# Bank 4 shared by two score products, output transposes first in a group, bursts of second scores of 3, 4 and 3

## The chip, the cores and the metric

The kernel runs on 1 core of one Trainium2 chip. The metric is the device time of one execution in microseconds (us). All arithmetic, inputs and outputs are float32 unless said otherwise. PE is TensorE, DVE VectorE, ACT ScalarE, POOL GpSimd and SP SyncE.

## The reference

Two layers over x of 4 batches, 512 tokens and 512 features. The change lies in the attention of the first layer, beside which the experts of the first layer's gate run:

```
x  = L0_attn_x                                   # (4, 512, 512)
xn = layernorm(x)
# attention: 32 heads of 16, 8 groups of keys and values (4 heads share one)
q, k, v = xn @ wq, xn @ wk, xn @ wv ; q, k rotated (rope)
scores = q k^T / sqrt(16) + causal mask
s = softmax(scores) v @ wo
# experts: each token's two best of 8
top_idx = top_k(xn @ W_gate + b_gate, 2)
g = silu(mean over the two of relu(xn @ W_e + b_e))
x = x + s * g
# second layer: an S4 convolution of 512 taps over the feature axis, times silu of a scaled linear layer
xn = layernorm(x)
x = x + s4(xn) * silu(xn @ w_deq^T + bias)
```

## The kernel before

The program has three stages. The first makes the layer norm, the projections and the routing of tokens to 39 expert tiles of 128 rows. The second, in which the change lies, runs attention group by group: a group (b, h) is one of 4 batches and one of 8 key-value heads with its 4 query heads, 32 groups in all. I number them 0 to 31 (8b + h). The third stage is the second layer.

**Scores are made twice.** *First scores* have queries as rows; VectorE adds the mask and takes each row's maximum (`maxima`, line 1400). These maxima are copied (`maxima_columns`, line 1409), turned by TensorE (`turn_maxima`, line 1640, "the turn"), split in two parts on VectorE (`maxima_rows`, lines 1417 and 1419) and stored as two more rows of the query operand. *Second scores* have keys as rows, with the maximum already subtracted in the product; ScalarE takes their exponentials (`exps`, line 1523), GpSimd clears what the causal mask excludes in diagonal blocks (`select`, line 1338), and TensorE multiplies with the values (`values`, line 1657).

A group has ten first scores (n = 0 to 9, line 1601) and ten second scores (n = 0 to 9, lines 1627 and 1630), each of them 512 columns into one PSUM bank. First score n is followed by maximum n, second score n by exponential n. A product uses 48 or 50 rows of the array, in one half of it or the other by n's parity, so that two products can run side by side; they are issued in turns, a first score of the *next* group and a second score of this one.

**Banks.** There are eight of 128 x 512. First scores rotate through three (0, 1, 5), second scores through three (2, 3, 6). Bank 4 takes the value products of a group and, in between, the turned maxima; bank 7 takes the expert and output products. First score n waits for maximum n - 3 and second score n for exponential n - 3, the readers of its bank.

**One group on TensorE**, written out in `pe_b`: burst one of first scores 3 to 6 of the next group with second scores 0 to 3 of this one; the quarters of gap 0; burst two of first scores 7 to 9 with second scores 4 to 6; up to three quarters of gap 1; the turn; the rest of gap 1; burst three of first scores 0 to 2 of the group after next with second scores 7 to 9; gap 2; the value products; gap 3. A *quarter* is one of four products of an expert tile (line 1685) or of an output tile (line 1696), two instructions. The numbers of quarters in the four gaps are (2, 4, 2, 0), (2, 3, 1, 0) or (2, 2, 2, 0) (`SIZES`).

**One group on VectorE**, in `dve_b`: maxima 3 to 6; the output transpose of the group before this one (`rows_of`, line 1430: it reads bank 4, where that group's value products have ended; it signals `b_o`); where h = 0 its division here (`divided`, lines 1435, 1439, 1447); maxima 7 to 9; the copy for the turn; elsewhere the division here; the two instructions behind the turn; then *expert transposes* (`expert_x`, line 1465, slot 0; each turns one tile of gathered token rows for its quarters); maxima 0 to 2 of the group after next; a piece of the S4 preparation (`dve_s4`); expert transposes of slot 1. The tables `TURNS` and `WORK` give the tiles: slot 1 holds one expert transpose in 17 of groups 1 to 29, two in groups 5, 10, 13, 18, 21 and 27, and none in the others.

**One group on ScalarE**, in `act_b`: exponentials 0 to 3, the eviction of a tile that ended in gap 0, exponentials 4 to 6, and so on. Every engine runs its own list in order and waits on semaphores: `b_m` counts maxima, `b_e` exponentials, `b_o` output transposes, `b_pv` the steps of value products.

## Time and profile before

| what | us |
| --- | --- |
| median of 3 runs | 658.91 |
| lowest and highest | 658.34, 660.49 |
| the profiled execution's own time | 656.67 |
| its span in the trace | 654.9 |
| TensorE busy, of the span | 605.2 |
| VectorE busy | 549.0 |
| ScalarE busy | 285.9 |

The profiled execution is one by itself, a little under the fastest of the timed runs; what is read from its trace is to be set against its own 656.67. The views of the trace used below give, for one stretch of time, each instruction or a few of a kind merged (with start and length), who waited for whom, and the busy time of each engine. An instruction whose idle time is shown in brackets was waited for by its engine, and the name behind the arrow is what released it.

### The profile page before, as it was taken

How to read it: one execution, taken by the hardware profiler on the slowest of the kernel's cores; microseconds unless marked ns; L12 is line 12 of the kernel's file. 1: busy time of each engine (PE TensorE's matmuls, PEld its weight loads, DVE VectorE, ACT ScalarE, POOL GpSimd, SP SyncE). 2: the span in 40 equal slices, each digit the busy share in tenths (PEclk: the TensorE clock that was granted, in tenths of full speed). 3: DMA queues.
4: the chain of work that ended last, by engine and by line, in shares of the span. 5: the costliest groups of instructions: out<-in, count | busy, mean ns of one | idle time of the engine just before them, and what ended most of it. 6: DMA issues, size and time to landing. Idle time of an engine off the chain costs nothing.

```text
span 654.9 us, 12411 instructions
## 1 busy us (share of the span) xinstructions
PE 605.2 (92%) x3541; PEld 348.9 (53%) x3565; DVE 549.0 (84%) x1789; ACT 285.9 (44%) x535; POOL 238.3 (36%) x364
## 2 busy tenths in 40 slices
PE   8899998968889999999999999998999999699997
PEld 5788784424444434444444444444444443388886
DVE  6698999867989979978988888997899957589994
ACT  4344324333345444534444534544454443445441
POOL 2767641332223133323221332212232116576620
PEclk9999999959999999999999999999999999889999
DMA  7599987665868643656742465644266328668841
GB/s 265 139 333 272 338 247 175 151 192 163 258 190 253 166 133 87 163 152 174 199 140 78 120 168 167 172 130 130 81 161 185 130 67 243 139 160 221 193 112 65
DMA packets 82880, 113.13 MB, mean 173 GB/s; under 512 B 12680, under 2 KB 45640, under 8 KB 82816
## 3 DMA queue, kind: packets, MB, share of 16 engines
q1 hardware_dynamic: 71074, 86.91, 44.8%
q0 software_dynamic: 6704, 18.62, 12.3%
q10 hardware_dynamic: 5038, 6.84, 4.2%
q8 instruction: 29, 0.48, 0.3%
q14 instruction: 35, 0.29, 0.2%
HBM read 72.15 MB, written 39.65 MB: 171 GB/s over the span
## 4 chain that ended last, share of the span: by engine, by line
PE 64%; DVE 20%; DMA 4%; issue 4%; POOL 2%; SPq 2%; ACT 2%; ACTq 1%; DVEq 0%; POOLq 0%
PE bank L1685 17%; DVE bank L1400 10%; PE bank L1027 8%; PE bank L1657 8%; PE bank L1601 7%; PE bank L2174 7%; PE bank L1696 5%; PE bank L2179 4%; DMA w_e<-expert_rows,slots 3%; PE bank L1627 2%; PE bank L1004 1%; DVE arena L1400 1%; ACTq L1321 1%; DVE arena L1465 1%; PE bank L2163 1%
## 5 line engine op out<-in xcount | busy, mean ns | idle before, releaser
L1400 DVE CUSTOM_DVE_ANT_0 bank<-bank,cst 128x384 f32<-128x384 f32 (+3 forms) x512 | 233.9, 522 | 37.5 <-PE bank L1601 35.1
L1523 ACT ACTIVATE arena<-bank 128x512 f32<-128x512 f32 x320 | 169.6, 602 | 147.8 <-PE bank L1627 113.9
L1338 POOL TENSOR_SCALAR_AFFINE_SELECT arena<-arena 128x512 f32<-128x512 f32 x128 | 80.5, 641 | 301.0 <-ACT arena L1523 301.0
L1685 PE MATMUL bank<-w_e,arena 128*128 x312 | 151.1, 609 | 7.5 <-DVE arena L1465 3.8
L1601 PE MATMUL bank<-kt,qt 48*128 48x512 f32 (+1 forms) x496 | 108.3, 336 | 13.1 <-DVE arena L1400 13.0
L1601 PEld LDWEIGHTS bank<-kt,qt 48*128 48x128 f32 x496 | 67.7, 187 | 80.2 <-DVE arena L1400 44.3
L1627 PE MATMUL bank<-qt,kt 50*128 50x512 f32 x256 | 93.7, 449 | 0.8 <-ACT arena L1523 0.4
L1685 PEld LDWEIGHTS bank<-w_e,arena 128*128 128x128 f32 x312 | 55.9, 192 | 52.0 <-issue 48.2
L1657 PE MATMUL bank<-arena 128*32 128x512 f32 (+3 forms) x1024 | 77.7, 441 | 0.0
L1400 DVE DVE_READ_ACCUMULATOR2_ANT arena<- 128x1 f32 x512 | 71.9, 140 | 0.0
L1696 PE MATMUL bank<-w_proj,arena 128*128 128x512 f32 x128 | 64.6, 629 | 0.8 <-ACT s_tok L1514 0.8
L1657 PEld LDWEIGHTS bank<-arena 128*32 128x32 f32 x1024 | 28.5, 110 | 50.5 <-issue 42.3
L1533 ACT ACTIVATE arena<-bank 128x512 f32<-128x512 f32 x39 | 23.4, 599 | 66.5 <-PE bank L1685 66.4
L1627 PEld LDWEIGHTS bank<-qt,kt 50*128 50x128 f32 x256 | 44.4, 186 | 4.7 <-ACT arena L1523 3.3
L1027 PE MATMUL bank<-proj_high,xh 128*128 128x264 f32 (+1 forms) x128 | 46.2, 361 | 0.4 <-DVE xl L527 0.4
L1027 PE MATMUL bank<-proj_low,xh 128*128 128x264 f32 (+1 forms) x128 | 43.5, 339 | 0.0
L1027 PE MATMUL bank<-proj_high,xl 128*128 128x264 f32 (+1 forms) x128 | 43.5, 339 | 0.0
L859 POOL TENSOR_TENSOR s_tok<-arena 128x256 f32<-128x256 f32 (+1 forms) x64 | 33.6, 555 | 25.8 <-DVE arena L546 20.2
L1350 POOL DMA_INDIRECT s_tok<-xn_rows,slots_i x39 | 38.1, 978 | 10.2 <-issue 5.2
L1696 PEld LDWEIGHTS bank<-w_proj,arena 128*128 128x128 f32 x128 | 22.5, 195 | 24.7 <-issue 20.5
L1924 POOL DMA_INDIRECT w_e<-expert_rows,slots x16 | 27.4, 1710 | 13.7 <-DMA w_e<-expert_rows,slots 10.5
L542 DVE TENSOR_TENSOR arena<-bank,cst 128x128 f32<-128x128 f32 (+1 forms) x63 | 27.1, 475 | 5.0 <-PE bank L1027 4.7
(168 smaller groups left out, 942.0 us busy)
## 6 DMA issues: line engine op xcount, KB each, us to landing
qt<-turned_parts SPq DMA_DIRECT2D x192, 64.0 KB, 2.7
turned_parts<-qk_parts SPq DMA_DIRECT2D x8, 1280.0 KB, 6.6
gathered_rows<-s_tok SPq DMA_DIRECT2D x39, 256.0 KB, 3.6
arena<-gathered_rows SPq DMA_DIRECT2D x39, 256.0 KB, 4.0
expert_rows<-arena SPq DMA_DIRECT2D x39, 256.0 KB, 2.3
w_e<-in_L_ffn_W_e ACTq DMA_DIRECT2D x24, 256.0 KB, 6.0
kt<-turned_parts SPq DMA_DIRECT2D x180, 32.0 KB, 2.7
arena<-in_L_attn_x SPq DMA_DIRECT2D x16, 256.0 KB, 6.0
```

Source lines behind the costliest of these rows:

```text
L859: i = g.tensor_tensor(o[:, :, :, c, :], xc[:, :, :, c, :], xs[:, :, :, 1 - c, :], op)
L1027: i = t.matmul(out[u % 2][:, 0:n], x[:, u % 2, k, :], w[part][:, k, :], start=(k == 0 and x is xh and part == 0), stop=(k == KB - 1 and pa ...
L1338: g.affine_select(out=diag, in_=diag, compare_op=ALU.is_ge, fill=0.0, base=0, pattern=[[0, 2], [0, HALF], [1, P]], channel_multiplier=-1). ...
L1350: e.indirect_dma_start(xr[m % 3], None, xn_d, bass.IndirectOffsetOnAxis(ap=slots_i[:, m:m + 1], axis=0)).then_inc(m_x[m % 3], 16)
L1400: i = v.tensor_tensor_reduce(out=part, in0=part, in1=const("mask")[:, S - w:], scale=1.0, scalar=LOWEST, op0=ALU.add, op1=ALU.max, accum_o ...
L1523: nc.scalar.activation(pt[:, s, first:second + 1:second - first].rearrange("p c r q -> p c (r q)"), s2_bank(b, h, n).rearrange("p (c x) -> ...
L1601: i = t.matmul(s1_bank(b, h, n)[:, at:at + w], stack[rows, x if r is None else r, q * P:w], kt[rows, h // 2 % 2, h % 2, 0:w], start=(x == ...
L1627: i = t.matmul(to, keys(j), queries[:, q:q + 2], start=True, stop=True)
L1657: i = nc.tensor.matmul(bank[4][VW * r:VW * (r + 1), j * P:], vb[:, j, h, :], pt[:, r // HALF, at:at + TPB - j, r % HALF, :], start=(j == O ...
L1685: i = t.matmul(bank[7], xgt[:, m % 2, k * P:(k + 1) * P], w_e[:, ex[m], k, :], start=False, stop=(k == KB - 1))
L1696: i = t.matmul(bank[to], ot[:, (b * PAIRS + k) % (PAIRS + 1), u, :], wo[:, k, :], start=(k == 0), stop=(k == KB - 1))
L2174: i = t.matmul(bank[2 + u % 2][:, :], x[:, u % 2, k, :], (w_high, w_low)[part][:, k, :], start=(k + n == 0), stop=(k + n == KB + 1))
```

## The change

Five edits, all in the second stage.

- First score 6 of a group (from the third group on) is written to bank 4 and no longer to its rotating bank. It waits for `b_o`, the output transpose of two groups back, in place of a maximum. The other first scores rotate over three banks without it, so those after it wait for maximum n - 4 in place of n - 3 (first scores 7 to 9), which in the rotation is again the reader of their bank.
- Second score 6 (in all groups but the first and the last) is written to bank 4 as well. It waits for maximum 6 of the next group. The second scores after it wait for exponential n - 4.
- The turn, which is written to bank 4 too, waits for exponential 6 besides.
- On VectorE the output transpose and behind it the expert transposes of the last group's slot 1 stand ahead of maxima 3 to 6. They stood behind maximum 6, and at the end of the last group.
- Second score 3 moves from burst one to burst two. ScalarE's eviction of the first gap's tile moves ahead of exponential 3.

```diff
         def s1_bank(b, h, n):
 
-            return S1_BANK[1 if (b, h) == (0, 0) else nth_of(NJ, b, h, n) % 3]
+            if (b, h) == (0, 0):
+                return S1_BANK[1]
+            if (b, h) == (0, 1):
+                return S1_BANK[(n + 1) % 3]
+            return bank[4] if n == 6 else S1_BANK[(n + 2 - (n > 6)) % 3]
 
         def s2_bank(b, h, n):
 
-            return S2_BANK[n % 2 if (b, h) == (0, 0) else nth_of(NJ, b, h, n) % 3]
+            if (b, h) == (0, 0):
+                return S2_BANK[n % 2]
+            if (b, h) == LAST_GROUP:
+                return S2_BANK[n % 3]
+            return bank[4] if n == 6 else S2_BANK[(n - (n > 6)) % 3]
...
+                    done, later = next_group(b, h, -1), h > 0 and following
+                    rows_of(*done)
+                    for m in TURNS.get((*done, 1), ()):
+                        expert_x(m)
                     if following:
                         for n in (3, 4, 5, 6):
                             maxima(e, *following, n)
-                    done, later = next_group(b, h, -1), h > 0 and following
-                    rows_of(*done)
                     if not later:
                         divided(*done)
...
-                    for m in TURNS.get((b, h, 1), ()):
-                        expert_x(m)
...
-                    for n in (0, 1, 2, 3):
+                    for n in (0, 1, 2):
                         exps(e, b, h, n)
                     results(b, h, 0)
-                    for n in (4, 5, 6):
+                    for n in (3, 4, 5, 6):
                         exps(e, b, h, n)
...
+        def second_burst(e, g1, g2):
+
+            scores_2(e, *g2, 3)
+            scores_2(e, *g2, 4)
+            scores_1(e, *g1, 7)
+            scores_1(e, *g1, 8)
+            scores_2(e, *g2, 5)
+            scores_2(e, *g2, 6)
+            scores_1(e, *g1, 9)
...
-            elif due(at := nth_of(NJ, b, h, n if alone_in_bank else n - 2)):
+            elif n == 6 and b * NG + h > 1:
+                e.wait_ge(b_o, nth_of(1, b, h, -1))
+            elif due(at := nth_of(NJ, b, h, n if alone_in_bank else n - 2 - (n > 6 and b * NG + h > 1))):
                 e.wait_ge(b_m, at)
...
-            elif due(at := nth_of(NJ, b, h, n - (1 if (b, h) == (0, 0) else 2))):
+            elif n == 6 and (b, h) not in ((0, 0), LAST_GROUP):
+                e.wait_ge(b_m, nth_of(NJ, b, h, NJ + 7))
+            elif due(at := nth_of(NJ, b, h, n - (1 if (b, h) == (0, 0) else 2) - (n > 6 and (b, h) not in ((0, 0), LAST_GROUP)))):
                 e.wait_ge(b_e, at)
...
             if due(at := nth_of(1, b, h, -1)):
                 e.wait_ge(b_o, at)
+            if b * NG + h > 1:
+                e.wait_ge(b_e, nth_of(NJ, b, h, 7 - NJ))
             t.transpose(turned_at(b, h), m_cols.rearrange("p s c x -> p (s c x)"), ident).then_inc(b_tm, 1)
...
-                    scores(e, (3, 4, 5, 6), following, (0, 1, 2, 3), (b, h))
+                    scores(e, (3, 4, 5, 6), following, (0, 1, 2), (b, h))
                     quarters(b, h, 0)
-                    scores(e, (7, 8, 9), following, (4, 5, 6), (b, h))
+                    second_burst(e, following, (b, h))
```

VectorE's order at the start of group 11, before. Line 671 is the end of group 10's S4 piece, line 1465 the expert transposes, the rows of line 1400 the maxima 3 (512 wide), 6 (384 and 128) and 7, line 1430 the output transpose; the rows left out are the readings and maxima 4 and 5:

```order
L671 TENSOR_TENSOR w_proj<-toep,arena 128x256 x2
L1465 STREAM_TRANSPOSE arena<-arena 128x4x4x32 x2
L1400 ISA bank0,arena<-bank0,cst 128x512
...
L1400 ISA bank0,arena<-bank0,cst 128x384
L1400 ISA arena 128x1
L1400 ISA bank0,arena<-bank0,cst 128x128
...
L1430 STREAM_TRANSPOSE arena<-bank4 128x512
L1400 ISA bank1,arena<-bank1,cst 128x384
```

The same place after the change, where line 1409 is what line 1400 was, 1439 the output transpose and 1474 the expert transposes:

```order
L671 TENSOR_TENSOR w_proj<-toep,arena 128x256 x2
L1439 STREAM_TRANSPOSE arena<-bank4 128x512
L1474 STREAM_TRANSPOSE arena<-arena 128x4x4x32 x2
L1409 ISA bank5,arena<-bank5,cst 128x512
...
L1409 ISA bank4,arena<-bank4,cst 128x384
L1409 ISA arena 128x1
L1409 ISA bank4,arena<-bank4,cst 128x128
...
L1409 ISA bank5,arena<-bank5,cst 128x384
```

The output transpose moved from behind maximum 6 to the front, and the two expert transposes now stand behind it; maximum 6 reads bank 4.

TensorE's order in group 11 before, from first score 6 on (line 1601; names ending in 67 are bank 6 or 7). Lines 1627 and 1630 are second scores, 1696 the two quarters of gap 0:

```order
L1601 MATMUL bank0<-kt,qt_56 128x384
L1601 MATMUL bank0<-kt,qt_56 128x128
L1627 MATMUL bank67<-qt_56,kt 128x512
L1696 MATMUL bank67<-w_proj,arena 128x512 x2
L1601 MATMUL bank1<-kt,qt_56 128x384
L1601 MATMUL bank1<-kt,qt_56 128x128
L1627 MATMUL bank2<-qt_56,kt 128x512
L1601 MATMUL bank5<-kt,qt_56 128x256 x2
L1627 MATMUL bank3<-qt_56,kt 128x512
L1601 MATMUL bank0<-kt,qt_56 128x256 x2
L1630 MATMUL bank67<-qt_56,kt 128x256 x2
```

The same place after, where 1601 is 1622, 1627 is 1650, 1630 is 1653 and 1696 is 1721:

```order
L1622 MATMUL bank4<-kt,qt_56 128x384
L1622 MATMUL bank4<-kt,qt_56 128x128
L1721 MATMUL bank67<-w_proj,arena 128x512 x2
L1650 MATMUL bank2<-qt_56,kt 128x512
L1650 MATMUL bank3<-qt_56,kt 128x512
L1622 MATMUL bank5<-kt,qt_56 128x384
L1622 MATMUL bank5<-kt,qt_56 128x128
L1622 MATMUL bank0<-kt,qt_56 128x256 x2
L1650 MATMUL bank67<-qt_56,kt 128x512
L1653 MATMUL bank4<-qt_56,kt 128x256 x2
L1622 MATMUL bank1<-kt,qt_56 128x256 x2
```

First score 6 and second score 6 now write bank 4, second score 3 stands in burst two, and second score 6 stands ahead of first score 9.

## Rows read from the trace of the kernel before

**Rows 1.** Stretches: length; busy PE, PEld, DVE, ACT, POOL; granted clock; DMA.

```profile
129.60:134.10 4.50, 3.63 (x22) 2.22 (x21) 4.50 (x19) 3.10 (x6) 1.58 (x2) 1.00 0.66 176
134.10:147.70 13.60, 8.14 (x30) 3.14 (x33) 6.94 (x26) 2.28 (x4) 3.77 (x5) 0.50 0.74 209
150.70:539.30 388.60, 361.76 (x2190) 171.09 (x2212) 340.91 (x1280) 179.50 (x342) 106.55 (x152) 1.00 0.53 153
```

**Rows 2.** Waits of 150.7 to 539.3: us in total, times, longest.

```profile
PE bank L1601 <- DVE arena L1400: 12.5, 29, 1.2
...
PE bank L1640 <- DVE arena L1409: 4.5, 12, 0.7
```

**Rows 3.** Timeline of TensorE, group 17: start, length, what, [idle before <- releaser].

```profile
354.07 0.51 PE L1657 MATMUL bank<-arena 128*32 128x384 f32 x4
354.51 0.49 PE L1601 MATMUL bank<-kt,qt 48*128 48x512 f32 x1
...
355.85 0.45 PE L1601 MATMUL bank<-kt,qt 48*128 48x384 f32 x1 [0.32 <-DVE arena L1400]
...
356.14 0.22 PE L1601 MATMUL bank<-kt,qt 48*128 48x128 f32 x1
356.28 1.98 PE L1696 MATMUL bank<-w_proj,arena 128*128 128x512 f32 x4
358.20 0.44 PE L1601 MATMUL bank<-kt,qt 48*128 48x384 f32 x1
...
358.54 0.44 PE L1627 MATMUL bank<-qt,kt 50*128 50x512 f32 x1
...
358.79 0.28 PE L1630 MATMUL bank<-qt,kt 50*128 50x256 f32 x1
...
358.94 0.27 PE L1601 MATMUL bank<-kt,qt 48*128 48x256 f32 x1
359.36 2.74 PE L1685 MATMUL bank<-w_e,arena 128*128 x6 [0.16 <-issue]
361.94 0.27 PE L1640 MATMUL bank<-cst,arena 128*128 128x128 f32 x1
```

**Rows 4.** Timeline of VectorE, the same group.

```profile
355.04 0.70 DVE L1400 CUSTOM_DVE_ANT_0 bank<-bank,cst 128x512 f32<-128x512 f32 x1 [1.46 <-PE bank L1601]
355.65 0.14 DVE L1400 DVE_READ_ACCUMULATOR2_ANT arena<- 128x1 f32 x1
...
357.95 0.14 DVE L1400 DVE_READ_ACCUMULATOR2_ANT arena<- 128x1 f32 x1
357.95 0.71 DVE L1430 STREAM_TRANSPOSE arena<-bank 128x512 f32<-128x512 f32 x1
358.73 0.57 DVE L1400 CUSTOM_DVE_ANT_0 bank<-bank,cst 128x384 f32<-128x384 f32 x1
...
361.17 0.18 DVE L1409 COPY arena<-arena 128x32 f32<-128x32 f32 x1
```

**Rows 5.** Timeline of TensorE in group 8: the start of burst one, and the turn.

```profile
232.85 0.50 PE L1601 MATMUL bank<-kt,qt 48*128 48x512 f32 x1
...
241.16 0.33 PE L1640 MATMUL bank<-cst,arena 128*128 128x128 f32 x1 [0.71 <-DVE arena L1409]
```

**Rows 6.** Timeline of VectorE at the start of group 11 (burst one at 272.01).

```profile
271.13 1.30 DVE L1465 STREAM_TRANSPOSE arena<-arena 128x512 f32<-128x512 f32 x2
```

**Rows 7.** Timeline of VectorE: maximum 7 in groups 6 (start 206.09) and 18 (366.39).

```profile
210.45 0.57 DVE L1400 CUSTOM_DVE_ANT_0 bank<-bank,cst 128x384 f32<-128x384 f32 x1 [0.21 <-PE bank L1601]
...
370.73 0.57 DVE L1400 CUSTOM_DVE_ANT_0 bank<-bank,cst 128x384 f32<-128x384 f32 x1
```

**Rows 8.** Timeline of VectorE in group 8: the division, and maximum 7.

```profile
237.15 0.26 DVE L1435 RECIPROCAL arena<-arena 128x16 f32<-128x16 f32 x1
...
238.53 0.53 DVE L1400 CUSTOM_DVE_ANT_0 bank<-bank,cst 128x384 f32<-128x384 f32 x1
```

**Rows 9.** The page: ScalarE's exponentials, busy us and mean ns of one.

```profile
L1523 ACT ACTIVATE arena<-bank 128x512 f32<-128x512 f32 x320 | 169.6, 602 | 147.8 <-PE bank L1627 113.9
```

1 line of the change is left out of this document (added).

## The prediction

> **What bounds the kernel now.** The page's busy shares say that TensorE and VectorE are the two full engines, and little more, so I read the stretches first: of the 388.6 us in which groups 2 to 30 run, TensorE is busy 361.8 and VectorE 340.9 [rows 1]. So both are nearly full there, and what counts is who waits for whom. The waits of that stretch name two places [rows 2]: a first score waits for VectorE's maxima in each of the 29 groups (12.5 us in all, at most 1.2), and the turn of the maxima waits 12 times (4.5 us). Then I laid one group out on both engines. I count time in a group from the start of its burst one; for group 17 that is 354.51 [rows 3], and "at 1.34" is meant so. It stands for the groups whose pace TensorE sets.
>
> Group 17 on TensorE [rows 3]: the value products of the group ahead end at 0.07, first score 6 starts at 1.34 after 0.32 idle, two quarters at 1.77, burst two at 3.69, its last product starts at 4.43, the next quarter at 4.85, the turn at 7.43. On VectorE [rows 4]: maximum 3 starts at 0.53, the last reading of maximum 6 ends at 3.58, the output transpose runs 3.44 to 4.15, maximum 7 starts at 4.22, the copy that the turn needs ends at 6.84. The turn comes 0.59 after it: here TensorE sets the pace. In group 8 (h = 0) the turn waits 0.71 for the copy [rows 5], and in groups with two quarters in gap 1 (6, 14, 18 and others) it waits less: there VectorE sets it.
>
> **What the change removes.** First score 6 waits for the output transpose in place of maximum 3. That transpose can start when the value products are done. VectorE started 0.04 after the TensorE result it needed (355.00 to 355.04), so at 0.11; it takes 0.71, end 0.82 [rows 3, 4]. TensorE answered VectorE's maximum 3 (355.79) after 0.06, so first score 6 starts at about 0.87 instead of 1.34. From there it is 0.43 to the quarters and 1.92 to burst two [rows 3], which so starts at 3.22 instead of 3.69. It has seven products now, not six; six took 0.74 from first start to last, half a pair more costs some 0.21, and the last would start at 4.17 instead of 4.43. **If nothing else waited, 0.26 us a group would be gained.** That second score 3 leaves burst one saves nothing, since it ran beside first score 6 and the quarters followed the latter.
>
> **What it adds.** Second score 6, in burst two, goes to bank 4 as well, and so must wait until VectorE has read first score 6 out of it. Ahead of that maximum VectorE now has the output transpose, and also the expert transposes that stood at the end of the group ahead. These were hidden: in group 11 two of them run 271.13 to 272.43, ahead of the maxima [rows 6]. Now they can't start before the value products end. One transpose lets the next instruction start after about 0.63 (two took 1.30, of which the last one's own 0.67) [rows 6]; from the start of maximum 3 to the last reading of maximum 6 are 3.05 [rows 4]. With x moved transposes, maximum 6 is read at 0.11 + 0.63 + 0.63x + 3.05 = **3.79 + 0.63x**. The product itself would be ready at 3.22 + 0.60 = 3.82. Queued behind it are the last first score, the quarters, the turn and the rest of the group, and VectorE itself waits for that turn; nothing gives the wait back. After a wait the second instruction of a product started 0.29 after the first (355.85, 356.14) [rows 3]. So the last product of burst two starts at 3.79 + 0.63x + 0.05 + 0.29:
> - x = 1: 4.76 against 4.43, a loss of 0.33.
> - x = 2: 5.39, a loss of 0.96.
> - x = 0: the wait is just over; 4.17.
>
> Bounds: with 0.12 in place of the restart of 0.29 (the nearest rows of products that didn't wait lie that close), each TensorE-set group loses 0.17 less; if the moved transpose pays a start of its own after its wait for a load, 0.1 more. I take the 0.29, as the row is of this very case, a product behind a VectorE wait.
>
> Where VectorE sets the turn, maximum 7 counts. It follows the last instruction of maximum 6, 0.08 ahead of the end of its reading, or comes at about 4.0, when its product is there.
>
> **The sum**, with x the number of expert transposes that the plan in the code puts at the end of the group ahead:
> - x = 1 and TensorE sets the turn: groups 5, 7, 9, 12, 13, 17, 20, 21, 23, 25, 29, 30. 12 by 0.33 = +4.0.
> - x = 1, but VectorE late already or setting the turn: 3, 4, 15, 27. In the first two maximum 3 started at 1.29 and 1.08 since the expert transpose was on the path before: 0.13 + 0.11 + 0.23 + 0.12 = +0.6.
> - x = 2 and TensorE sets the turn: 11, 19. 2 by 0.96 = +1.9.
> - x = 2 and VectorE sets it: 6 and 28, where maximum 7 moves from 4.36 [rows 7] to 4.97, +0.61 each; by the same reckoning 14 (from 4.63) +0.34, and 22 (from 5.24, VectorE late already) -0.18. +1.4.
> - x = 0, h = 0: 8, 16, 24. Between the maxima stands the division, 1.42 from one start to the next. Maximum 7 starts at 0.11 + 0.63 + 2.97 + 1.42 = 5.13 instead of 5.68 [rows 5, 8], and the turn had waited for it: 3 by -0.55 = -1.65.
> - x = 0 otherwise: 10, 18, 26. Maximum 7 from 4.34 [rows 7] to about 4.02, when its product is there; in 10 VectorE is free only at 0.24: -0.18 - 0.31 - 0.31 = -0.8.
> - Group 2: its value products end 1.8 ahead of the burst, so all transposes lie in idle time: -0.36. Group 1: the turn is set by VectorE's work, the same in either order: 0. Group 31 has no first scores to wait: 0.
>
> Together 4.0 + 0.6 + 1.9 + 1.4 - 1.65 - 0.8 - 0.36 = **+5.1 us**.
>
> Costed at nothing: the turn now also waits for exponential 6. At x = 2 second score 6 ends at about 5.7 and an exponential takes 0.60 [rows 9], so 6.3, and the turn is at 7.6; with x = 0 all is 1.3 earlier. Each us past the turn would be a us. The eviction of the first gap's tile stands one exponential earlier on ScalarE, and burst two covers it. SyncE's load of the next expert tile waits for the moved transpose, up to 2 us later in the group, and its tile is used a group later. One more wait stands ahead of the turn; it costs between nothing and about 0.1 in the 12 groups where the turn waits for VectorE, and is in the range only.
>
> The profiled execution took 656.67, its span 654.9; with the change that is 661.8. It was 2.2 below the median of the runs shown, so the forecast for a median is 658.91 + 5.1 = **664.0 us**.
>
> On the pairs: pair starts in a burst lie some 0.24 to 0.35 apart [rows 3], and before the change two products in a row often used the same half of the rows; now the halves alternate all through burst two. The Trainium skill ("TensorE: Matmul & The Clock Gate", Part 3, The mechanism) says that weight loads overlap running matmuls only where the row group differs. By that rule the new burst two would close up, by 0.1 a group as my estimate from the 0.34 between its first two pair starts and the 0.24 of the next. In groups with x of 1 or 2 the wait swallows it, so by the rule the sum is 0.6 lower, and by the rows as above.
>
> **Rivals.**
> 1. *The wait for maximum 6 is hidden* (faster). It decides where maximum 6 is read by 3.82 even with x = 1, that is if VectorE is 0.6 quicker than its rows. Then the 12 groups gain 0.26 each (-3.1), 3, 4 and 15 some 0.4 each (-1.2), 11 and 19 lose only 0.2 each at the turn, and the rest stays as above (27 +0.1, x = 2 +1.4, the others -2.8): about -5.2, 653.7 us. For it: the 12.5 us of waiting do go, and VectorE has idle time. Against it: that idle time lies ahead of the value products' end, where the moved transposes can't be any more. 0.10.
> 2. *The same mechanism, smaller.* With 0.12 for the restart in 14 groups (-2.4) and the closer pairs (-0.6), +2: about 661 or less, which is within 0.3%, the least that a measurement of this kernel can tell. 0.16.
> 3. *The clock, or a second wait.* TensorE's granted clock stood at 0.50, its 1.2 GHz level, in 134.1 to 147.7, and TensorE was busy for 8.1 of those 13.6 us, after 3.6 of the 4.5 ahead of them; in groups 2 to 30 it was 1.00 [rows 1]. A second such stretch would cost 4 us (its busy work at full speed took half) to 7 us (half the stretch): 668 to 671. The new wait is a piece of idle of up to 1.3 us. Against it: a wait of 1.2 stood in a group before [rows 2] and the clock held. The Trainium skill ("TensorE: Matmul & The Clock Gate", HAM oscillation) has TensorE's idle between pieces of work bring the clock down; by that rule groups 6, 11, 19 and 28 are where it would show. With other losses as large, such as a GpSimd gather behind a delayed store: 0.14.
>
> **Numbers.** Forecast 0.60, rivals 0.10, 0.16, 0.14. The low end takes in rival 2 and runs as low as the lowest before, 659.5. The high end adds to the forecast 1.2 for the waits, 1.6 by which the highest run of before lies over the median, and 0.8 for the moved transposes' own start: 667.5. Faster 0.10, same 0.16, slower 0.74.
>
> **What would show it.** First scores wait for VectorE's maxima for under 2 us, not 12.5. A new wait stands at second score 6 (line 1653 after) for VectorE: about 0.6 with x = 1, 1.3 with x = 2, some 14 us in all. The turn is at 7.8 in group 17, 8.4 in group 11, 7.8 in group 8. It would be wrong if maximum 6 is read before burst two gets there, if the turn doesn't follow burst two by the same distance, or if something behind the turn waits anew.

## The result, and the profile after

The changed kernel took 666.88 us (median of 4 runs, 666.05 to 668.55) beside 659.20 for the kernel before on the same chip: a ratio of 1.0111, 95% interval 1.0079 to 1.0143. It is slower, as forecast, and 2.9 us above the forecast median of 664.0, inside the range. The profiled execution took 666.05 with a span of 664.3 (656.67 and 654.9 before). Measured twice more, on two chips, the same kernel gave 1.0062 (1.0043 to 1.0080) and 1.0075 (1.0047 to 1.0103); the forecast was 664.0 / 658.91 = 1.0077. So the change itself costs about what was forecast, and the first measurement holds more: some 3 us by the ratio, 3.8 us in its trace, which the sections below place but don't explain.

Lines of the code after stand 9 to 25 further down than before: the maxima are L1409, the output transpose L1439, the expert transpose L1474, the exponentials L1532, a first score L1622, a second score L1650 (512 columns) and L1653 (256 or 128, second score 6 among them), the turn L1665, the value products L1682, the quarters L1710 and L1721.

Stretches of the changed kernel, with the columns of [rows 1]: group 1, and groups 2 to 30.

```profile
131.70:151.70 20.00, 13.22 (x70) 6.20 (x70) 12.15 (x45) 5.33 (x10) 5.34 (x7) 0.74 0.70 192
151.70:547.70 396.00, 373.00 (x2189) 175.20 (x2211) 335.89 (x1279) 179.34 (x341) 106.56 (x152) 1.00 0.52 150
```

The loss is in the second line: 396.00 us where [rows 1] had 388.60, +7.4, at the same granted clock of 1.00. Ahead of it, stage 1 came out 2.1 us longer (untouched work) and group 1 1.1 us shorter; behind it the tail is 1.0 longer. VectorE is busy for 5 us less in a stretch that is 7.4 longer, so it waits more. TensorE is busy for 11.2 us more with the same work. The end of a product is modelled and can cover a part of a wait: second score 6, which starts at 3.90 in groups 8, 16 and 24, which have no moved transposes, starts at 4.49 in group 17, and only 0.15 of that shows as idle (the lines below). So what a wait costs is read here from the starts of instructions, not from busy or idle time.

Waits of 150 to 545 in the changed kernel: us in total, times, longest.

```profile
DVE arena L1439 <- PE bank L1682: 38.7, 26, 4.0
...
PEld bank L1653 <- DVE arena L1409: 13.1, 22, 1.1
...
PE bank L1653 <- DVE arena L1409: 6.2, 22, 0.8
...
PE bank L1622 <- DVE arena L1439: 4.3, 8, 1.2
...
PE bank L1665 <- DVE arena L1418: 2.2, 7, 0.4
```

The 12.5 us in which first scores waited for maxima [rows 2] are gone. Second score 6 (L1653) now waits for maxima in 22 groups: 6.2 us in which TensorE computes nothing, 13.1 us on its weight loads. The prediction's "some 14 us in all" is the row of the weight loads. VectorE waits 38.7 us for value products ahead of the output transpose. And first scores wait 4.3 us for that transpose. By these rows alone TensorE waits less than before (6.2, 4.3 and 2.2 against 12.5 and 4.5), though the stretch is 7.4 longer; that is why the positions within a group follow.

Timelines of group 17, TensorE and then VectorE, to be laid beside [rows 3, 4]; its burst one starts at 359.00.

```profile
359.00 0.50 PE L1622 MATMUL bank<-kt,qt 48*128 48x512 f32 x1
...
360.40 1.99 PE L1721 MATMUL bank<-w_proj,arena 128*128 128x512 f32 x4
362.31 0.50 PE L1650 MATMUL bank<-qt,kt 50*128 50x512 f32 x2
...
363.49 0.38 PE L1653 MATMUL bank<-qt,kt 50*128 50x256 f32 x1 [0.15 <-DVE arena L1409]
...
363.71 0.27 PE L1653 MATMUL bank<-qt,kt 50*128 50x256 f32 x1
...
366.74 0.27 PE L1665 MATMUL bank<-cst,arena 128*128 128x128 f32 x1
```

```profile
359.20 0.72 DVE L1439 STREAM_TRANSPOSE arena<-bank 128x512 f32<-128x512 f32 x1 [1.86 <-PE bank L1682]
359.84 0.67 DVE L1474 STREAM_TRANSPOSE arena<-arena 128x512 f32<-128x512 f32 x1
360.43 0.67 DVE L1409 CUSTOM_DVE_ANT_0 bank<-bank,cst 128x512 f32<-128x512 f32 x1
...
363.30 0.14 DVE L1409 DVE_READ_ACCUMULATOR2_ANT arena<- 128x1 f32 x1
```

Burst two starts at 3.31 (3.69 before), so the old wait is gone. But the transposes push maximum 3 from 0.53 to 1.43, maximum 6 is read at 4.44, and second score 6 starts 0.05 later, at 4.49. The last product starts at 4.71 to 4.73 and the turn at 7.74, against 4.43 and 7.43.

Groups 11 (two moved transposes, burst one at 274.90) and 8 (none, at 235.01) on TensorE: second score 6 and the turn, and the turn alone.

```profile
279.98 0.38 PE L1653 MATMUL bank<-qt,kt 50*128 50x256 f32 x1 [0.76 <-DVE arena L1409]
...
283.22 0.27 PE L1665 MATMUL bank<-cst,arena 128*128 128x128 f32 x1
```

```profile
242.72 0.33 PE L1665 MATMUL bank<-cst,arena 128*128 128x128 f32 x1 [0.38 <-DVE arena L1418]
```

In group 11 the wait is 0.76 and the turn comes at 8.32; in group 8, at 7.71 where [rows 5] had 8.31.

**Six late groups.** Group by group all this agrees with the forecast, except in 5, 10, 13, 18, 21 and 27. There the output transpose starts at 0.55, 1.48, 0.55, 1.43, 0.56 and 0.66 instead of 0.19. Group 10 (burst one at 261.49): VectorE, ScalarE and GpSimd.

```profile
262.96 0.72 DVE L1439 STREAM_TRANSPOSE arena<-bank 128x512 f32<-128x512 f32 x1 [1.24 <-PE bank L1682]
```

```profile
262.98 1.08 ACT L1532 ACTIVATE arena<-bank 128x512 f32<-128x512 f32 x2 [2.63 <-PE bank L1650]
```

```profile
259.91 0.99 POOL L1359 DMA_INDIRECT s_tok<-xn_rows,slots_i  x1 [0.15 <-issue]
261.21 0.95 POOL L1359 DMA_INDIRECT s_tok<-xn_rows,slots_i  x1 [0.30 <-issue]
```

The last value product ended at 261.56, yet VectorE and ScalarE, each released by a different product of TensorE, both started at 262.96 to 262.98. These six are the groups ahead of which GpSimd issues two gathers back to back. "Two in a row" is not the only thing that sets them apart: in the other groups with a gather the last one starts 1.57 us or more ahead of burst one, in these six 0.07 to 1.24, and in all six the output transpose starts 1.5 to 1.8 us after the second gather does (261.21 to 262.96 here). A delay that long behind a gather would be over in the other groups. In the profile of the kernel before there is no such delay in group 10 (burst one at 259.64), where ScalarE and VectorE wait for TensorE too:

```profile
260.21 1.57 ACT L1523 ACTIVATE arena<-bank 128x512 f32<-128x512 f32 x3 [1.71 <-PE bank L1627]
```

ScalarE starts at 0.57 there (1.49 in the changed kernel), and at 0.57 in group 18 (1.44). In the other groups a delay to 0.66 could hardly be seen, and that execution, 656.67 us long, was faster than every timed run of its set (658.34 to 660.49); so it doesn't tell whether the kernel before is free of it.

To compare kernels I use a sum that leaves out groups 2 and 22, the two that change most between executions of one kernel: the lengths of **the 26 groups** 3 to 21 and 23 to 29 (from one burst one to the next). Each sum is from one profiled execution. Groups 3 and 7 still change by up to 0.8 and 0.5 us between executions of one kernel. The 26 groups take 347.15 us in the kernel before and 355.23 in this profile of the changed one.

### The profile page after: what moved, and what is told of

The parts are those of the page before. It is cut to its first block, busy times and chain, and to the rows that moved or that the text cites. A ratio compares the mean times of both kernels' runs of the same rounds, so it can differ in the third digit from the quotient of the medians.

```text
span 664.3 us, 12405 instructions
## 1 busy us (share of the span) xinstructions
PE 617.6 (93%) x3541; PEld 354.5 (53%) x3565; DVE 545.4 (82%) x1789; ACT 286.7 (43%) x535; POOL 239.3 (36%) x364
## 4 chain that ended last, share of the span: by engine, by line
PE 52%; DVE 27%; DMA 7%; issue 6%; POOL 2%; ACT 2%; SPq 2%; ACTq 1%; DVEq 0%; POOLq 0%
DVE bank L1409 14%; PE bank L1710 13%; PE bank L1682 10%; PE bank L2199 7%; PE bank L1027 4%; PE bank L2204 4%; DMA turned_parts<-qk_parts 3%; DVE arena L1474 3%; PE bank L1721 3%; DMA w_e<-expert_rows,slots 3%; PE bank L1622 2%; DVE arena L1409 2%; PE bank L1653 2%; PE bank L983 1%; ACTq L1330 1%
## 5 line engine op out<-in xcount | busy, mean ns | idle before, releaser
L1409 DVE CUSTOM_DVE_ANT_0 bank<-bank,cst 128x384 f32<-128x384 f32 (+3 forms) x512 | 231.7, 520 | 7.1 <-PE bank L1622 6.6
L1532 ACT ACTIVATE arena<-bank 128x512 f32<-128x512 f32 x320 | 169.5, 603 | 150.2 <-PE bank L1650 114.6
L1710 PE MATMUL bank<-w_e,arena 128*128 x312 | 151.2, 609 | 8.0 <-DVE arena L1474 5.0
L1622 PE MATMUL bank<-kt,qt 48*128 48x512 f32 (+1 forms) x496 | 103.3, 333 | 4.3 <-DVE arena L1439 4.3
L1622 PEld LDWEIGHTS bank<-kt,qt 48*128 48x128 f32 x496 | 66.9, 187 | 48.6 <-issue 33.7
L1650 PE MATMUL bank<-qt,kt 50*128 50x512 f32 x256 | 84.1, 449 | 1.0 <-DMA qt<-m_rows 0.5
L1710 PEld LDWEIGHTS bank<-w_e,arena 128*128 128x128 f32 x312 | 55.5, 192 | 53.0 <-issue 49.0
L1682 PE MATMUL bank<-arena 128*32 128x512 f32 (+3 forms) x1024 | 76.6, 436 | 0.0
L1409 DVE DVE_READ_ACCUMULATOR2_ANT arena<- 128x1 f32 x512 | 70.8, 138 | 0.0
L1721 PE MATMUL bank<-w_proj,arena 128*128 128x512 f32 x128 | 64.0, 623 | 0.8 <-ACT s_tok L1523 0.8
L1439 DVE STREAM_TRANSPOSE arena<-bank 128x512 f32<-128x512 f32 x32 | 22.9, 716 | 41.5 <-PE bank L1682 41.4
L1682 PEld LDWEIGHTS bank<-arena 128*32 128x32 f32 x1024 | 28.2, 109 | 49.3 <-issue 41.0
L1650 PEld LDWEIGHTS bank<-qt,kt 50*128 50x128 f32 x256 | 39.2, 186 | 27.4 <-issue 22.7
L1653 PE MATMUL bank<-qt,kt 50*128 50x256 f32 x128 | 31.6, 330 | 7.1 <-DVE arena L1409 6.2
L1721 PEld LDWEIGHTS bank<-w_proj,arena 128*128 128x128 f32 x128 | 22.1, 192 | 24.2 <-issue 20.1
```

The source lines that it names most:

```text
L1409: i = v.tensor_tensor_reduce(out=part, in0=part, in1=const("mask")[:, S - w:], scale=1.0, scalar=LOWEST, op0=ALU.add, op1=ALU.max, accum_o ...
L1532: nc.scalar.activation(pt[:, s, first:second + 1:second - first].rearrange("p c r q -> p c (r q)"), s2_bank(b, h, n).rearrange("p (c x) -> ...
L1622: i = t.matmul(s1_bank(b, h, n)[:, at:at + w], stack[rows, x if r is None else r, q * P:w], kt[rows, h // 2 % 2, h % 2, 0:w], start=(x == ...
L1650: i = t.matmul(to, keys(j), queries[:, q:q + 2], start=True, stop=True)
L1653: i = t.matmul(to[:, x * HALF * P:(x + 1) * HALF * P], keys(j), queries[:, q], start=(x == 0), stop=True, skip_group_check=True)
L1682: i = nc.tensor.matmul(bank[4][VW * r:VW * (r + 1), j * P:], vb[:, j, h, :], pt[:, r // HALF, at:at + TPB - j, r % HALF, :], start=(j == O ...
```

## The experiments

All ratios are to the kernel before on the same chip, which took 656.12 us in the first set, 655.30 in the second, 656.63 in the third and 659.06 in the last.

### The changed kernel again, twice

> The changed kernel itself once more, to see whether what its first trace showed comes again. In that trace groups 2 to 29 took 7.4 us more than before, and 4 of them stood in six groups (5, 10, 13, 18, 21, 27) in which the signal of the last value product reached VectorE 0.3 to 1.3 us late, so that the output transpose started at 0.55, 1.48, 0.55, 1.43, 0.56 and 0.66 of the group and not at 0.20. Theory A (the delay belongs to the program: GpSimd issues two gathers back to back at the end of exactly the groups ahead of these six): the same six groups show the same starts to within 0.1 us, and the time is 666 to 668 us. Theory B (a chance of that execution): other groups or none, and groups 2 to 29 then take 3.5 us more than before and not 7.4.

Measured: 660.90 us, ratio 1.0062 (1.0043 to 1.0080). The output transposes of the six groups start at 0.19 to 0.27; the 26 groups take 351.36 us. Groups 2 to 29 took 5.3 us more than before, where theory B had 3.5. The difference is group 2, 15.05 us long at a lower clock (see the last section) where the later profile has 13.37.

> The changed kernel unchanged, once more. Its first measurement gave a ratio of 1.0111 [1.0079, 1.0143] and a profile with six groups in which the output transpose began 0.3 to 1.3 us late; its second 1.0062 [1.0043, 1.008] and a profile with none of the six. Reading one (chance of an execution or a day's chip): ratio 1.005 to 1.008, groups 2 to 29 at 378 to 380 us, no late start in the six, perhaps one elsewhere. Reading two (belongs to the change, met in some executions): ratio 1.009 to 1.012 and late starts again in those same groups, groups 2 to 29 at 381 us or more.

Measured: 660.68 us, ratio 1.0075 (1.0047 to 1.0103), the six at 0.19 to 0.28, the 26 groups 351.48. Here is group 10 of the later profile (burst one at 260.42), VectorE, ScalarE, GpSimd:

```profile
260.70 0.72 DVE L1439 STREAM_TRANSPOSE arena<-bank 128x512 f32<-128x512 f32 x1
```

```profile
260.99 1.57 ACT L1532 ACTIVATE arena<-bank 128x512 f32<-128x512 f32 x3 [1.71 <-PE bank L1650]
```

```profile
258.85 0.99 POOL L1359 DMA_INDIRECT s_tok<-xn_rows,slots_i  x1 [0.15 <-issue]
260.15 0.95 POOL L1359 DMA_INDIRECT s_tok<-xn_rows,slots_i  x1 [0.30 <-issue]
```

The two gathers lie where they did, within 0.01 us of burst one, and nobody is late. So the gathers alone don't make it (something else must differ between the measurements), and the late starts were 3.8 us of the first profile's 26 groups (355.23 against 351.4). The change's own cost there is 351.4 - 347.15 = +4.3.

### The expert transposes back at the group's end

```diff
                     rows_of(*done)
-                    for m in TURNS.get((*done, 1), ()):
-                        expert_x(m)
...
                         numerators(e, st, h - 2)
+                    for m in TURNS.get((b, h, 1), ()):
+                        expert_x(m)
```

> The change with one part undone: the expert transposes of slot 1 stand again at the end of their group; the output transposes stay ahead of the maxima. Theory 1 (the prediction: they hold back maximum 6 and with it second score 6, on which the rest of the group waits): where x was 1 or 2 maximum 6 is read at about 3.85 and not at 4.43 and 5.02, second score 6 starts at 3.9, and by the same reckoning groups 2 to 30 take 7 us less than the changed kernel: 660 us, as before the change or 0.6 over it, if the value products' signals stay late in six groups, and 656 if they don't. Rival (what costs is bank 4 and its waits, whoever stands ahead on VectorE): at most 2 us less than the changed kernel, 665 to 667 us.

Measured: 654.45 us, ratio 0.9963 (0.9936 to 0.9990); the 26 groups 342.21 us, 9.2 less than the changed kernel and 4.9 less than before. Group 17 (burst one at 353.31), TensorE:

```profile
357.14 0.50 PE L1653 MATMUL bank<-qt,kt 50*128 50x256 f32 x2
...
360.55 0.27 PE L1665 MATMUL bank<-cst,arena 128*128 128x128 f32 x1
```

The whole time is 6.5 us less than the changed kernel's and 1.7 less than before (medians of the same set). The ten runs of this kernel had a mean granted clock of 0.981 and the 19 of the kernel before 0.986, so part of what the groups gain seems to be lost again to more time at the lower clock; why there is more of it is open.

No idle time of TensorE is left ahead of second score 6, which starts at 3.84 right behind the reading of maximum 6 (3.79). The turn comes at 7.25. The steps of the forecast for x = 0 (3.79, turn some 0.26 earlier than 7.43) hold for the groups that TensorE sets and that had one moved transpose (turn at 7.23 to 7.27, in 29 at 7.34). In 11 and 19, which had two, these now end only after burst one has begun, the output transpose starts at 0.34 and the turn comes at 7.39. The place of the expert transposes is necessary for the loss as the change stands.

### The gather later in GpSimd's queue

```diff
+                    if b * NG + h > 0:
+                        next_gather(*next_group(b, h, -1), 2)
                     next_gather(b, h, 0)
...
-                    next_gather(b, h, 2)
```

> The changed kernel with GpSimd's gathers that stood behind the last select of a group now behind the first select of the next one, at 1.8 to 4 of a group, far from the value products. Theory A (two gathers in a row while VectorE stands waiting for the value products' signal hold TensorE's signals back): no output transpose starts later than 0.25 except where VectorE is late by itself (groups 3 and 4), groups 10 and 18 are 1.2 us shorter each, 5, 13, 21 by 0.35 and 27 by 0.45, together 4 us: 662.5 to 663.5 us. Theory B (the lateness has another cause): the six late starts stay, 666 to 668 us. If the later gathers hold up GpSimd's selects or a load of an expert tile, another group gets longer.

Measured: 669.85 us, ratio 1.0189 (1.0162 to 1.0215), but for a reason of its own: the first gathers are late, and group 1 waits for its expert tile (27.14 us long instead of 19.90). The stretch 130.00 to 151.20 in this kernel, then in the changed kernel's second profile, columns as in [rows 1]:

```profile
130.00:151.20 21.20, 7.68 (x39) 4.20 (x39) 10.70 (x43) 5.55 (x10) 7.44 (x9) 0.68 0.56 152
```

```profile
130.00:151.20 21.20, 14.89 (x80) 6.94 (x80) 12.93 (x48) 5.83 (x12) 5.35 (x7) 0.76 0.72 190
```

As no late start was met on that chip in any kernel, it says nothing of the late starts. A wasted run: the control should have been seen to be late first.

### The wait of the output transpose in two instructions

```diff
-                e.wait_ge(b_pv, nth_of(4, b, h, 4))
                 if due(at := nth_of(1, b, h, 0)):
                     e.wait_ge(b_on, at)
+                alone(e)
+                e.wait_ge(b_pv, nth_of(4, b, h, 4))
```

`alone` is a nop that keeps the wait ahead of it out of the next instruction.

> The changed kernel with one edit on VectorE: the wait ahead of the output transpose, which in the trace is one instruction that stands waiting for two semaphores (the value products' and VectorE's own), is split, so that the transpose carries the wait for the value products alone. Theory A1 (it is this standing double wait, together with the gathers, that holds TensorE's signals back): the starts of the output transposes in groups 5, 10, 13, 18, 21 and 27 go to 0.2, 662.5 to 663.5 us; all others start 0.05 to 0.1 earlier too. Theory A2 (the gathers do it with any kind of wait): the six stay late, 666 to 668 us.

Measured: 662.44 us, ratio 1.0077 (1.0050 to 1.0103), the same as the changed kernel in the whole time. In the trace the transposes start at 0.14 instead of 0.19, the turn of group 17 at 7.67 instead of 7.73, and the 26 groups take 350.45 instead of 351.4. So the split is worth 0.05 us in those groups. It isn't a price that every wait for two semaphores pays: with the wait unsplit the transpose starts at 0.14 too in group 30 of the changed kernel, and in x_back's groups that have one expert transpose just ahead of it (17, for one). In groups 3, 4, 10 and 22 the split made it 0.10 later.

### The second scores' old banks, with the rest of the change

```diff
         def s2_bank(b, h, n):
-            if (b, h) == (0, 0):
-                return S2_BANK[n % 2]
-            if (b, h) == LAST_GROUP:
-                return S2_BANK[n % 3]
-            return bank[4] if n == 6 else S2_BANK[(n - (n > 6)) % 3]
+            return S2_BANK[n % 2 if (b, h) == (0, 0) else nth_of(NJ, b, h, n) % 3]
...
-            elif n == 6 and (b, h) not in ((0, 0), LAST_GROUP):
-                e.wait_ge(b_m, nth_of(NJ, b, h, NJ + 7))
```

> The changed kernel, but the second scores keep the three banks in turn that they had before the change, so second score 6 waits for an exponential and not for maximum 6. All else of the change stays: first score 6 in the value products' bank, output and expert transposes ahead of the maxima, bursts of 3, 4 and 3. Theory (the loss is the wait of second score 6 for maximum 6): with that wait gone the twelve groups with one expert transpose have their last product of burst two at 4.2 to 4.3 us and the turn of the maxima at 7.25 to 7.3 instead of 7.73, groups 11 and 19 the turn at 7.3 to 7.5 instead of 8.33; groups 2 to 29 take about 370 us instead of 379.5 (374.3 in the kernel before), and the time is 8 us or more under the changed kernel's 660.9, some 652 to 654 us. Rival A (VectorE's longer work before maximum 3 is itself the cost, since later maxima run late): the turn stays at 7.6 or later and the time within 2 us of 660.9. Rival B (the exponential becomes the new wait of second score 6): a wait of the second scores for ScalarE of more than 5 us over groups 2 to 29, and groups 2 to 29 at 374 to 377 us.

Measured: 660.39 us, ratio 1.0070 (1.0042 to 1.0099); the 26 groups 351.20. My theory, as I put it there, fell, and rival B's wait is in the trace: 6.1 us, groups 2 to 29 in 377.70 (B had up to 377). Rival A's two numbers came out as well (turn at 7.79, time within 2 us); against it speaks that the turn still comes 3.01 after the last product of burst two, so that VectorE's later maxima don't set it. The waits of 150 to 545, group 17 on TensorE (burst one at 358.88), and ScalarE there:

```profile
PEld bank L1647 <- ACT arena L1528: 15.2, 29, 0.5
...
PE bank L1647 <- ACT arena L1528: 6.1, 29, 0.2
```

```profile
363.43 0.39 PE L1647 MATMUL bank<-qt,kt 50*128 50x256 f32 x1 [0.23 <-ACT arena L1528]
...
366.67 0.27 PE L1657 MATMUL bank<-cst,arena 128*128 128x128 f32 x1
```

```profile
362.29 0.59 ACT L1519 COPY s_tok<-bank 128x512 f32<-128x512 f32 x1 [1.27 <-PE bank L1713]
362.78 2.07 ACT L1528 ACTIVATE arena<-bank 128x512 f32<-128x512 f32 x4
```

With three banks in turn, second score 6 takes the bank of second score 3. Before the change these two were in different bursts; now they are in the same one, so TensorE has to wait until exponential 3 has read the bank, and that exponential can only follow its own product in the same burst: it starts at 3.90, 0.59 after second score 3 (3.30), where exponential 0 starts 0.57 after second score 0. The eviction ahead of it (362.29) therefore costs 0.03 at most. Second score 6 starts at 4.55, no earlier than with its wait for maximum 6 (4.49).

### The new bursts alone

The kernel before, with bursts of 3, 4 and 3 second scores and the eviction ahead of exponential 3; on TensorE:

```diff
-                    scores(e, (3, 4, 5, 6), following, (0, 1, 2, 3), (b, h))
+                    scores(e, (3, 4, 5, 6), following, (0, 1, 2), (b, h))
                     quarters(b, h, 0)
-                    scores(e, (7, 8, 9), following, (4, 5, 6), (b, h))
+                    second_burst(e, following, (b, h))
```

> The kernel before with one part of the change alone: bursts of 3, 4 and 3 second scores instead of 4, 3 and 3, so second score 3 moves from burst one to burst two, and on ScalarE the evacuation of results goes ahead of exponential 3. Banks and VectorE's order are those of before. It tells what the seventh product of burst two costs by itself, which my sum had at 0.21 us. Theory (burst one is filled by its wait for the output transpose, so a product taken out of it gives nothing back, and the seventh in burst two costs 0.21 in each group that TensorE sets, 12 to 17 of them): +2.5 to +3.5 us. Rival (first score 6 starts by as much earlier as burst one is shorter, the two cancel): 0 within 1 us.

Measured: 673.17 us, ratio 1.0271 (1.0223 to 1.0319); the 26 groups 360.54, +13.4, where both theories had 3.5 or less. Group 17 on TensorE (burst one at 361.31):

```profile
366.25 0.38 PE L1640 MATMUL bank<-qt,kt 50*128 50x256 f32 x1 [0.23 <-ACT arena L1523]
...
369.50 0.27 PE L1650 MATMUL bank<-cst,arena 128*128 128x128 f32 x1
```

The same wait for exponential 3: second score 6 at 4.94 instead of 4.28, the turn at 8.18 instead of 7.43. So moving second score 3 with the other edits left out costs 0.75 a group, not 0.21, and the bank that the change gives second score 6 is what pays for it. The exponential again starts 0.59 after its product (4.28 and 3.69), so the moved eviction isn't the reason.

### Both put back: the fourth corner

The two diffs above together: expert transposes at the group's end, second scores in their old banks.

> The changed kernel with the expert transposes back at the end of the group and, with that, the second scores in the three banks in turn of before. With the kernel after, the expert transposes alone put back (groups 2 to 29 in 370.9 us) and the banks alone put back (377.7) it makes a square of four. New theory (two waits stand side by side at second score 6: maximum 6 if it goes to the value products' bank, exponential 3 if it shares a bank with second score 3, which now is in the same burst; the later one decides): second score 6 at 4.5 to 4.55 us in the groups that TensorE sets although maximum 6 is read at 3.79, last product at 4.75, turn of the maxima at 7.75 to 7.8, and groups 2 to 29 at 376 to 378 us, time 659 to 661; nothing of the 8.6 us that the expert transposes gave back alone. Rival (the exponential was late only because maximum 3 and what follows were late): second score 6 at 3.9 to 4.1, groups 2 to 29 at 370 to 372 us, time 653 to 655.

Measured: 662.74 us, ratio 1.0085 (1.0052 to 1.0119); the 26 groups 351.59. Group 17 (burst one at 358.13), TensorE:

```profile
362.63 0.38 PE L1647 MATMUL bank<-qt,kt 50*128 50x256 f32 x1 [0.22 <-ACT arena L1528]
...
365.87 0.27 PE L1657 MATMUL bank<-cst,arena 128*128 128x128 f32 x1
```

Second score 6 at 4.50 and the turn at 7.73, although the transposes are out of the way. The whole time and groups 2 to 29 (380.23) lie 2 us over the forecast; group 22, which the sum leaves out, took 15.23 at a lower clock. The square, in us for the 26 groups:

| | second score 6 in the value products' bank | old banks in turn |
|---|---|---|
| expert transposes ahead of the maxima | 351.4 (the change) | 351.2 |
| at the group's end | **342.2** | 351.6 |

Of two waits at one instruction the later decides. They happen to end within 0.06 us of each other (4.49 and 4.55), so taking away either alone gives nothing, and the 9 us of these groups (6.5 in the whole time) come only where both are short. The ratios of the four say the same: 1.0062 and 1.0075, 1.0070, 0.9963, 1.0085.

### x_back with the split wait

> The changed kernel with the expert transposes back at the end of the group, and with the wait for the value products in an instruction of its own, so that the output transpose has one semaphore to wait for and not two. The expert transposes at the group's end alone gave 654.45 us, a ratio of 0.9963 to the kernel before, and groups 2 to 29 at 370.9 us. Theory: the split starts the output transpose 0.05 us earlier in each group (0.14 to 0.09, or 0.14 still if that is already when the signal comes), which moves maximum 6, second score 6 and the turn by as much in the twelve groups that TensorE sets: 0 to -0.6 us, a ratio of 0.995 to 0.9965. Rival (the added instruction delays VectorE elsewhere): +1 us or more.

Measured: 653.43 us, ratio 0.9963 (0.9939 to 0.9987); the 26 groups 342.07 against 342.21. The groups that TensorE sets had their output transpose at 0.14 already; only groups without moved transposes (8, 16, 18, 24, 26) gain their 0.05.

### VectorE's wait for the value products in the kernel before

```diff
+                    prior = next_group(b, h, -1)
+                    e.wait_ge(b_pv, nth_of(4, *prior, 4))
+                    if due(at := nth_of(1, *prior, 0)):
+                        e.wait_ge(b_on, at)
+                    alone(e)
                     if following:
                         for n in (3, 4, 5, 6):
                             maxima(e, *following, n)
```

> The kernel before, with VectorE waiting ahead of maximum 3 of each group for the value products' signal and for the evacuation of results, although maximum 3 needs neither. It tells apart two readings of the late starts that one profiled execution of the changed kernel had in groups 5, 10, 13, 18, 21 and 27 and a later execution had not. Reading one (TensorE's signals of the value products come late by chance, and in the kernel before nothing stood behind them at that place): single groups begin maximum 3 0.3 to 1.3 us later than 0.53, in some executions. Reading two (late signals belong to the change's own order): no group is late. The price of the wait with every signal on time is 0 to 0.05 us a group, under 1.5 us in all, because maximum 3 waits for its scores until 0.53 anyway.

Measured: 654.93 us, ratio 0.9990 (0.9962 to 1.0018), the 26 groups 346.54 against 347.15: such a wait costs nothing when the signals are on time. No group was late, but that chip had no late starts in any kernel, so this leaves the question open.

### The best version: two parts of the change alone

The kernel before, with the output transpose first (its wait split as above) and first score 6 in the value products' bank. Bursts, second scores' banks, ScalarE's order and the expert transposes as before:

```diff
+            return bank[4] if n == 6 else S1_BANK[(n + 2 - (n > 6)) % 3]
...
+                    done, later = next_group(b, h, -1), h > 0 and following
+                    rows_of(*done)
                     if following:
                         for n in (3, 4, 5, 6):
                             maxima(e, *following, n)
-                    done, later = next_group(b, h, -1), h > 0 and following
-                    rows_of(*done)
...
+            elif n == 6 and b * NG + h > 1:
+                e.wait_ge(b_o, nth_of(1, b, h, -1))
...
```

> The kernel before with two parts of the change alone: the output transpose first in the group (with the wait for the value products in an instruction of its own), and first score 6 in the value products' bank. Bursts of 4, 3 and 3, the banks of the second scores, the order on ScalarE and the place of the expert transposes are those of before. Theory: first score 6 starts at 0.91 instead of 1.34, all of burst two comes 0.43 earlier (start 3.26, last product 4.00), no second score waits for a maximum or for an exponential of its own burst, and the turn comes at 7.02 instead of 7.43 in the groups that TensorE sets, 0.21 earlier than with x_back (7.23); VectorE could be ready at 4.02 + 2.67 = 6.69. Groups 2 to 29: 370.9 less 12 to 14 times 0.21, so 368 us, time 650 to 652, a ratio of 0.990 to 0.993, the fastest so far. Rival (VectorE or the exponentials become the bound before the turn, the seventh product of burst two was hidden): turn at 7.2 or later, groups 2 to 29 at 370.5 to 372, a ratio of 0.996.

Measured: 650.89 us, ratio 0.9909 (0.9874 to 0.9943): the time that the theory named, with a mechanism that was wrong in one step. The turn of group 17 comes at 7.32, not 7.02, and the 26 groups take 342.61. TensorE there (burst one at 354.65):

```profile
355.87 0.50 PE L1635 MATMUL bank<-qt,kt 50*128 50x512 f32 x1
356.30 1.98 PE L1704 MATMUL bank<-w_proj,arena 128*128 128x512 f32 x4
358.21 0.44 PE L1609 MATMUL bank<-kt,qt 48*128 48x384 f32 x1
...
361.97 0.27 PE L1648 MATMUL bank<-cst,arena 128*128 128x128 f32 x1
```

The quarters start at 1.65. In the kernel before it took 0.43 from first score 6 to them, here 0.74: second score 3 (355.87) used to fill the 0.29 between the two pieces of first score 6 after its wait [rows 3], and without the wait there is no such gap. So second score 3 costs 0.31 in burst one here, and the new bursts with bank 4 are worth only 0.07 to 0.09 a group (turn at 7.23 to 7.25 against 7.32). By the 26 groups this version and x_back are equal within 0.5 us; by their intervals (0.9874 to 0.9943, and 0.9936 to 0.9990) I can't call it faster.

> The same kernel as in the run named old_bursts (output transpose first, first score 6 in the value products' bank, all else as before), once more with five rounds. It measured 0.9909 [0.9874, 0.9943] there, and the two with the expert transposes put back 0.9963 with intervals that end at 0.9936 and 0.9939. By groups 2 to 29, and leaving out the groups 2 and 22, the three take as long as each other within 1 us, so the theory is that the true ratio lies between: 0.990 to 0.995, groups 2 to 29 at 369 to 370 us, the turn of the maxima at 7.31 again. Rival (the first measurement had luck): 0.995 to 0.998.

Measured on a fourth chip: 655.26 us, ratio 0.9916 (0.9889 to 0.9944), against 659.06 for before; groups 2 to 29 in 373.58, where 369 to 370 was expected. Both measurements lie below 1 with all of their intervals: output transpose first and one bank changed are worth 0.6 to 1.3%. And on this chip the late starts are back, in the same six groups: 0.50, 1.39, 0.46, 1.39, 0.55 and 0.63 in groups 5, 10, 13, 18, 21 and 27. Group 10 (burst one at 261.13), VectorE, ScalarE and GpSimd:

```profile
262.52 0.72 DVE L1436 STREAM_TRANSPOSE arena<-bank 128x512 f32<-128x512 f32 x1 [1.15 <-PE bank L1665]
```

```profile
262.58 0.60 ACT L1529 ACTIVATE arena<-bank 128x512 f32<-128x512 f32 x1 [2.59 <-PE bank L1635]
```

```profile
259.56 0.99 POOL L1355 DMA_INDIRECT s_tok<-xn_rows,slots_i  x1 [0.15 <-issue]
260.86 0.95 POOL L1355 DMA_INDIRECT s_tok<-xn_rows,slots_i  x1 [0.30 <-issue]
```

This kernel has neither the moved expert transposes, nor the new bursts, nor the second scores' new bank. So the late starts don't need those, and a chance of single executions is unlikely: the same six groups, in two kernels, in the first measurement and on this chip, and in none of the ten profiles on the three chips between that could have shown them. Here too the output transpose starts 1.5 to 1.8 us after the second gather does. In the two sets that show them the kernel before took 659.2 and 659.1 us, in the others 655.3 to 656.6, so it is some 3 us slower there as well. What delays these starts on such a chip is open; so is whether the kernel before loses its 3 us by the same, since its waiting variant wasn't run on such a chip.

## Why the prediction was right, point by point

**The bound, and the wait that goes.** Right: first scores no longer wait for maxima, burst two starts at 3.31 (I had 3.22). The term was 0.09 off, since the output transpose starts at 0.19 and not at 0.11. I had taken the 0.04 with which VectorE answered one product of TensorE; here it answered after 0.12, of which splitting the wait in two instructions took away 0.05.

**The wait that comes.** Right in place and mechanism: second score 6 for maximum 6, in 22 groups. 3.79 + 0.63x gave 4.42 for x = 1, read 4.44; for x = 2, 5.05, read 5.03. Two errors cancel: the start was 0.08 later, the transposes 0.64 and 0.59 apart and the maxima 0.04 shorter. The restart was 0.23 and not 0.29, so the last product starts at 4.72 (4.76 forecast) and 5.31 (5.39). Without the wait (x = 0) maximum 6 was read at 3.84 and the last product started at 4.28, where I had 4.17.

**The sum**, from the changed kernel's third profile, which has no late starts, as the change of the turn against the kernel before (groups 2 and 4: of the length):

| groups | forecast each | measured each |
|---|---|---|
| x = 1, TensorE sets the turn (12) | +0.33 | +0.28 to +0.30, in 30 +0.21 |
| 11, 19 (x = 2) | +0.96 | +0.85, +0.88 |
| 6, 28 | +0.61 | +0.56, +0.57 |
| 14; 22 | +0.34; -0.18 | +0.29; -0.29 |
| 8, 16, 24 | -0.55 | -0.60 |
| 10; 18 and 26; 2 | -0.18; -0.31; -0.36 | -0.18; -0.25; -0.35 |
| 15; 3; 4; 27 | +0.23; +0.13; +0.11; +0.12 | +0.17; +0.04; +0.02; +0.10 |

That adds up to +3.7 us where the forecast had +5.1; the whole lengths of groups 2 to 29 differ by +3.7 (377.96 against 374.28). That the turn follows burst two at a fixed distance was right: 3.00 before, 3.01 after. In 8, 16 and 24 the forecast used 1.42 from one start to the next over the division; [rows 8] give 238.53 - 237.15 = 1.38, and with that the term is -0.59, as measured.

**What the sum missed.** The first measurement's +7.4 in groups 2 to 30 is this +3.7 and the 3.8 of the late starts. I had costed the output transpose's new wait at the plain latency of a signal, because no row of the kernel before had VectorE waiting for TensorE between the gathers and burst one. That the first result lay in the range is luck in this part: the range went up for other reasons (1.2 for waits, 0.8 for the transposes' own start). Its low end of 659.5 is called the lowest before; that was 658.34.

**A step that was right only in company.** The prediction had 0.21 for the seventh product, and nothing saved by second score 3 leaving burst one. The runs show that the move costs 0.75 without the other edits (a wait for exponential 3), that the new bank of second score 6 removes that wait, and that leaving burst one saves 0.31 as soon as first score 6 doesn't wait. None of it changes the sum, as all parts of the change are there at once; but a reader who took the parts for independent would have dropped the bank, and lost 9 us (x_back against the fourth corner, 342.2 and 351.6).

**The rivals.** Rival 1 (the wait hidden) needed x = 0 ahead of the maxima: with the expert transposes back it is what happens, at 654.45. Rival 2 (smaller) is what the two later measurements look like, ratios of 1.0062 and 1.0075, though by other terms than its 0.12 restart. Rival 3 (the clock) didn't decide the first result: the granted clock over groups 2 to 30 was 1.00 after as before. In the second profile a small piece of it is there (group 2).

**On the pairs of scores.** The Trainium skill ("TensorE: Matmul & The Clock Gate", Part 3, The mechanism) led me to expect burst two to close up by 0.1 us a group. Group 2 is where its seven products run without a wait in between (maximum 6 is read at 3.58): in the third profile burst two starts at 3.22 (154.22 less 151.00) and second score 6 at 3.81, and the last product at 4.23, so 1.0 us from first start to last, where I had 0.74 + 0.21 = 0.95 from the rows. The trace doesn't show the 0.1; the rows were nearer.

## What to carry to other kernels

When a buffer is moved to remove a wait, list for the new buffer everything that must have left it, and what its reader's engine has queued ahead: here 0.6 us of hidden transposes, moved ahead of that reader, turned a gain of 5 us in the 26 groups into a loss of 4. Where two waits stand at one instruction, taking away either alone can measure as nothing; only the square of four kernels shows what each is worth. And before asking what causes an event that comes and goes between chips, get the unchanged kernel to show it on the chip in use.
